# Graph layer on one core: row and node one-hots in one VectorE instruction, row one-hots widened by ScalarE

## The chip, the cores and the metric

The kernel runs on one core of a Trainium2 chip. The metric is the device time of one execution in microseconds (us). The core has TensorE (PE, with its weight loads shown apart as PEld), VectorE (DVE), ScalarE (ACT), GpSimd (POOL) and SyncE (SP), and 16 DMA engines that all of them feed.

## The reference, cut to what matters

6250 nodes with 256 features, 200000 weighted edges. A layer norm is followed by a sum over edges (the part that the change touches), an attention-like product and, after a second layer norm, a mixture of eight experts:

```
xn = layernorm(x)
msgs = edge_weight[:, None] * xn[dst]            # for each edge, a row of 256
agg = segment_sum(msgs, src, num_segments=6250)  # added up by node
x = x + agg + mix(xn)
x = x + moe(layernorm(x))
```

## The kernel before

The stages run one after another: the norm, the mix, the edge stage, the routing, the experts. The edge stage takes some 1350 us of the 1988.

The edges are cut into 7 rounds (`q`, NQ = 7), and within a round each of 49 steps (`b`, NB = 49) treats one block of 128 nodes; a step has the number `t = q * 49 + b`. For a step there are six tiles of up to 128 edges. Three (GN) have rows of `xn` fetched by GpSimd, one indirect DMA each (L1285). Three (DN) have edges whose rows lie close together, in a window of 128 rows that is already in SBUF. Every tile is turned into a matrix product: a one-hot of the edge's node times its weight says to which node the row goes.

What the engines do in step `t`:

- VectorE makes the one-hots of the step (`one_hots`). L1440 compares the numbers 0 to 127, each written twice side by side in PSUM (`slots_of`), with the node of each edge (`recb`, six numbers a step and partition): 6 x 128 bf16, `hots`. L1445 compares the same numbers, fp32 in PSUM, with the row of each edge within its window (`recd`, three a step): 3 x 128 fp32, `row_hots`. Both write one of two buffers, by `t % 2`. L1458 (`finish`) adds the finished product of an earlier step to the node's sum.
- ScalarE (`weigh`, L1388) multiplies the six node one-hots by the edge weights, one instruction each, bf16 to fp32, into `weighted`. It also moves the window products from PSUM to SBUF (`keep`, L1379).
- TensorE makes `ap`, the row one-hots times the weighted node one-hots (L1338, which needs `weighted_done`), then the products of the fetched rows (L1351, which needs the gathers and VectorE's `summed` of two steps before), then those of the windows (L1355, which needs ScalarE's `a_kept`).
- GpSimd may be up to five steps (AHEAD) in front of TensorE.

In rounds 1 to 6 the next round is also sorted beside the products (`bins`): VectorE counts and places edges (`dve_share`; among it L445, L489, L511 and L513), TensorE multiplies what it made (L392), ScalarE moves the result (L405). At the end of a round `dve_decode` writes `recb`, `recd` and `scale` for the next one (L579 to L581). In the last round the sorting is gone, and the second layer norm and the routing run beside the products.

The order on every engine is that of the code. VectorE's turn in step `b` is: one-hots of step `b + 1`, then L1458 for step `b - 2`, then its share of the sorting. ScalarE's turn is: `keep` of step `b`, then `weigh` of step `b + 1`. Before the one-hots VectorE waits for two events, so that the buffer that it overwrites has been read: `a_done` (TensorE has used `row_hots`) and `weighted_done` (ScalarE has used `hots`).

Of the kernel before, what the change touches and what calls it, by code (L numbers as in the profile page):

```python
# [12 lines left out]
ALU = mybir.AluOpType  # L13
# [3 lines left out]
P = 128  # L17
# [12 lines left out]
NB = NT  # L30
# [76 lines left out]
class Bins:  # L107
# [4 lines left out]
    FARTHEST = 254  # L112
    NE = SC
    assert NE % 2 == 0
    HALVES = 2 * CB
# [20 lines left out]
    def __init__(self, nc, st, above, iota49, iota128, part, ident, low_i):  # L136
# [43 lines left out]
        self.recb = st.sb("recb", [P, NB, NE], BF16)  # L180
        self.recd = st.sb("recd", [P, NB, DN])
        self.scale = st.sb("scale", [P, NB, SC])
# [93 lines left out]
    def dve_consts(self, dve):  # L276
        nc = self.nc
        nc.vector.memset(self.ones[:, :], 1.0)
        nc.vector.memset(self.ones_f[:, :], 1.0)
        nc.vector.memset(self.offset[:, 0, :], 0.0)  # L280
        nc.vector.memset(self.merged[:, :, GN, :], 0)
        for i in range(2):
            nc.vector.tensor_copy(self.iota128b[:, :, i], self.iota128[:, :])
            last = nc.vector.tensor_copy(self.iota49b[:, :, i], self.iota49[:, :])
        self.link(dve, last)
# [286 lines left out]
    def dve_decode(self, dve, q):  # L572
        nc = self.nc

        if q > 0:
            dve.wait_ge(self.weighted_done, q * NB)
        for a, b, node, weight in ((0, GN, self.merged[:, 1, 0:GN, :], self.merged[:, 2, 0:GN, :]),
                                   (GN, SC, self.src_of[:, KG:CB, :], self.weight_of[:, KG:CB, :])):
            nc.vector.tensor_copy(self.recb[:, :, a:b], node.rearrange("p k b -> p b k"))  # L579
            nc.vector.tensor_copy(self.scale[:, :, a:b], weight.bitcast(F32).rearrange("p k b -> p b k"))  # L580
        nc.vector.tensor_scalar_add(self.recd[:, :, :], self.dst_of[:, KG:CB, :].rearrange("p k b -> p b k"), -1.0)\  # L581
            .then_inc(self.decoded, 1)
        dve.wait_ge(self.decoded, q + 1)
        assert self.links == self.LINKS, self.links
# [582 lines left out]
def edge_stage(nc, xn_dram, sum_dram, low_i, flag, h, ident, iota128, bins, router_w, rwT, logits, hn_dram):  # L1167


    with Stage(nc, "edge") as st:  # L1170
        NE, AHEAD = bins.NE, 5
        recb, recd, scale = bins.recb, bins.recd, bins.scale
        most1 = st.sb("most1", [P, 1])
# [5 lines left out]
        hots = st.sb("hots", [P, 2, NE // 2, P, 2], BF16)  # L1179
        row_hots = st.sb("row_hots", [P, 2, DN, P])  # L1180
        weighted = st.sb("weighted", [P, 2, SC, P])
# [60 lines left out]
        with nc.Block() as block:  # L1242
# [128 lines left out]
            def _(act):  # L1371
# [9 lines left out]
                def weigh(q, b):  # L1381
# [3 lines left out]
                    if t >= 2:  # L1385
                        act.wait_ge(stepped, t - 1)
                    for i in (*range(GN, SC), *range(GN)):
                        last = nc.scalar.activation(weighted[:, t % 2, i, :], hots[:, t % 2, i // 2, :, i % 2], ACT.Copy,  # L1388
                                                    scale=scale[:, b, i:i + 1])
# [43 lines left out]
            def _(dve):  # L1433
                def one_hots(q, b):

                    t = q * NB + b
                    if t >= 2:
                        dve.wait_ge(a_done, t - 1)
                        dve.wait_ge(weighted_done, t - 1)
# [3 lines left out]
                        recb[:, b, :].rearrange("p (t a h) -> p t a h", a=1, h=2).to_broadcast([P, NE // 2, P, 2]),  # L1443
                        ALU.is_equal)
                    nc.vector.tensor_tensor(  # L1445
                        row_hots[:, t % 2, :, :],
                        rows_of_window[:, :].rearrange("p (a s) -> p a s", a=1).to_broadcast([P, DN, P]),
                        recd[:, b, :].rearrange("p (c a) -> p c a", a=1).to_broadcast([P, DN, P]),
                        ALU.is_equal).then_inc(hot_done, 1)
# [976 lines left out]
```

## Time and profile before

| what | value |
|---|---|
| median of three runs | 1996.81 us (1991.59 to 1999.81) |
| the profiled execution | 1989.69 us, its span 1988.0 us |
| busy share PE / PEld / DVE / ACT / POOL | 89% / 77% / 69% / 55% / 65% |
| GpSimd's gathers L1285 | 1029, from 271.2 us on |
| mean granted TensorE clock | 0.956 of 2.4 GHz |

A row of a timeline gives the start of an instruction or of a merged row of like ones, how long it took, engine, line, operation, what is written and read, the count, and in brackets how long the engine had been idle and what ended that. A row of a group gives the count, the busy time, the mean of one in ns, and the idle time of the engine just before them. Matmuls are pipelined, so the starts of weight loads (PEld) are used here to tell when TensorE gets to a piece of work.

### The profile page before, as it was taken

The numbers are of one execution on the slowest core, as the hardware profiler recorded it, in microseconds if no ns is written. First come the engines' busy times: TensorE is split into PE (matmuls) and PEld (weight loads), VectorE is DVE, ScalarE is ACT, GpSimd is POOL, SyncE is SP. The second block draws the span as 40 slices with busy tenths as digits, with TensorE's granted clock in tenths as the row PEclk, the third lists the DMA queues.
The fourth block names the chain that finished last, engine by engine and source line by source line (L and its number), as shares of the span: only waits on it lengthen the run. The fifth ranks groups of instructions, "written<-read, shape, count | busy, mean of one in ns | idle before, by whom it ended". The sixth has DMA issues, their size and how long they took to land. (4 is left out here: it accounts for less than half of the span.)

```text
span 1988.0 us, 33518 instructions
## 1 busy us (share of the span) xinstructions
PE 1764.5 (89%) x10522; PEld 1527.8 (77%) x10522; DVE 1380.9 (69%) x2880; ACT 1093.2 (55%) x3267; POOL 1286.6 (65%) x1283
## 2 busy tenths in 40 slices
PE   5677878999899989998999999999999983999994
PEld 3366667988798889887988898889899972787773
DVE  6988458886888798788878986988677768010113
ACT  5632025556555655565556555655576652776662
POOL 1000367777777777777777777777777740777773
PEclk9988889999999999999999999999999986999997
DMA  7522453443233323332333333333344432344557
GB/s 255 196 87 95 138 173 122 139 131 117 91 107 104 112 91 106 105 112 90 105 105 108 93 107 104 104 99 104 106 133 133 136 109 70 102 144 131 164 161 228
DMA packets 130054, 244.30 MB, mean 123 GB/s; under 512 B 26533, under 2 KB 77620, under 8 KB 129880
## 3 DMA queue, kind: packets, MB, share of 16 engines
q0 software_dynamic: 59584, 161.78, 26.9%
q1 hardware_dynamic: 63852, 73.97, 11.4%
q10 hardware_dynamic: 6444, 6.40, 0.9%
q8 instruction: 89, 1.46, 0.3%
q14 instruction: 85, 0.70, 0.1%
HBM read 197.24 MB, written 45.77 MB: 122 GB/s over the span
## 5 line engine op out<-in xcount | busy, mean ns | idle before, releaser
L1285 POOL DMA_INDIRECT edge_G<-xn_scratch,edge_row_i x1029 | 1031.7, 1003 | 313.5 <-issue 290.6
L1388 ACT ACTIVATE edge_weighted<-edge_hots,bins_scale 128x128 f32<-128x128 bf16 x2058 | 638.5, 391 | 66.6 <-DVE edge_row_hots L1445 65.3
L1351 PE MATMUL edge_op<-edge_G,edge_weighted 128*128 128x256 f32 x2058 | 523.9, 391 | 62.1 <-DVE all_xn L1458 36.7
L1379 ACT COPY edge_A<-edge_ap 128x384 f32<-128x384 f32 x343 | 164.1, 478 | 533.1 <-PE edge_ap L1338 533.1
L1351 PEld LDWEIGHTS edge_op<-edge_G,edge_weighted 128*128 128x128 f32 x2058 | 366.7, 191 | 111.2 <-DVE all_xn L1458 50.7
L1440 DVE TENSOR_TENSOR edge_hots<-edge_numbers,bins_recb 128x768 bf16<-128x768 bf16 x343 | 190.6, 556 | 194.2 <-PE edge_ap L1338 190.0
L1338 PEld LDWEIGHTS edge_ap<-edge_weighted,edge_row_hots 128*128 128x128 f32 x2058 | 278.7, 192 | 39.1 <-issue 14.2
L1338 PE MATMUL edge_ap<-edge_weighted,edge_row_hots 128*128 128x128 f32 x2058 | 287.5, 276 | 11.6 <-ACT edge_weighted L1388 8.7
L1355 PE MATMUL edge_op<-bins_win,edge_A 128*128 128x256 f32 x1176 | 289.9, 383 | 0.0
L1355 PEld LDWEIGHTS edge_op<-bins_win,edge_A 128*128 128x128 f32 x1176 | 226.8, 193 | 31.9
L1355 PE MATMUL edge_op<-edge_win,edge_A 128*128 128x256 f32 x882 | 218.4, 384 | 0.0
L2320 DVE SCALAR_TENSOR_TENSOR exp_acc<-exp_ys,ffn_share,all_xn 128x256 f32<-128x256 f32 (+1 forms) x49 | 20.6, 481 | 248.9 <-DMA exp_ys<-ys_scratch 246.8
L1355 PEld LDWEIGHTS edge_op<-edge_win,edge_A 128*128 128x128 f32 x882 | 170.6, 193 | 24.2
L1445 DVE TENSOR_TENSOR edge_row_hots<-edge_numbers,bins_recd 128x384 f32<-128x384 f32 x343 | 187.8, 548 | 0.0
L1080 POOL TENSOR_TENSOR all_xn<-mix_xg,mix_qbias 128x1024 f32<-128x1024 f32 (+1 forms) x13 | 29.0, 2228 | 188.8 <-DVE mix_xg L1158 187.7
L392 PE MATMUL bins_bp<-bins_RH,bins_SL 128*128 128x147 bf16 x1582 | 142.0, 232 | 8.5 <-DVE bins_SL L513 8.0
L2184 POOL DMA_INDIRECT exp_xt<-hn_scratch,ffn_token x105 | 103.0, 981 | 71.6 <-POOLq L2007 40.0
L1458 DVE TENSOR_TENSOR all_xn<-all_xn,edge_op 128x256 f32<-128x256 f32 (+1 forms) x343 | 140.9, 411 | 9.0 <-PE edge_op L1355 8.8
L392 PEld LDWEIGHTS bins_bp<-bins_RH,bins_SL 128*128 128x128 bf16 x1582 | 122.4, 99 | 12.8 <-DVE bins_SL L513 7.5
L2190 POOL DMA_INDIRECT ys_scratch<-exp_yt,ffn_target x105 | 108.0, 1028 | 32.3 <-issue 28.3
L2239 PE MATMUL exp_dn<-ffn_w2s,exp_gT 128*128 x420 | 120.1, 409 | 0.0
L2226 PE MATMUL exp_up<-exp_xT,exp_w1x 128*128 128x128 f32 x840 | 113.6, 279 | 0.1
(343 smaller groups left out, 2080.2 us busy)
## 6 DMA issues: line engine op xcount, KB each, us to landing
edge_G<-xn_scratch,edge_row_i POOLq DMA_INDIRECT x1029
exp_ys<-ys_scratch SPq DMA_DIRECT2D x12, 1024.0 KB, 6.4
ln_xin<-in_x SPq DMA_DIRECT2D x12, 512.0 KB, 5.3
xn_scratch<-ln_xnb ACTq DMA_DIRECT2D x12, 512.0 KB, 6.3
xnT_scratch<-ln_xT SPq DMA_DIRECT2D x12, 512.0 KB, 6.8
mix_xg<-xn_scratch SPq DMA_DIRECT2D x12, 512.0 KB, 3.8
mix_ek<-xnT_scratch SPq DMA_DIRECT2D x12, 512.0 KB, 4.7
mix_xg<-in_x SPq DMA_DIRECT2D x12, 512.0 KB, 3.9
```

The source lines that it names most:

```text
L392: last = nc.tensor.matmul(self.bp[:, 0:self.NV * NB], self.SL[:, s % 2, t - a, :, side], self.R[:, s % 2, t - a, :, :, side].rearrange("p ...
L1285: pool.indirect_dma_start(out=G[:, t % AHEAD, i, :], out_offset=None, in_=xn_dram, in_offset=bass.IndirectOffsetOnAxis(ap=row_i[:, q % 2, ...
L1338: last = nc.tensor.matmul(ap[j][:, i * P:(i + 1) * P], row_hots[:, j, i, :], weighted[:, j, GN + i, :], start=True, stop=True)
L1351: nc.tensor.matmul(op[j][:, :], weighted[:, j, i, :], G[:, rb, i, :], start=i == 0, stop=False)
L1355: last = nc.tensor.matmul(op[j][:, :], A[:, j, i, :], win[q % 2][:, i, :], start=False, stop=i == DN - 1)
L1379: nc.scalar.copy(A[:, j, :, :].rearrange("p c s -> p (c s)"), ap[j][:, :]).then_inc(a_kept, 1)
L1388: last = nc.scalar.activation(weighted[:, t % 2, i, :], hots[:, t % 2, i // 2, :, i % 2], ACT.Copy, scale=scale[:, b, i:i + 1])
L1440: nc.vector.tensor_tensor(hots[:, t % 2, :, :, :], bins.slots_of[:, :, :].rearrange("p (a s) h -> p a s h", a=1).to_broadcast([P, NE // 2, ...
L1445: nc.vector.tensor_tensor(row_hots[:, t % 2, :, :], rows_of_window[:, :].rearrange("p (a s) -> p a s", a=1).to_broadcast([P, DN, P]), recd ...
L1458: nc.vector.tensor_tensor(h[:r, b, :], h[:r, b, :], op[(q * NB + b) % 2][:r, :], ALU.add).then_inc(summed, 1)
L2226: last = nc.tensor.matmul(up[t % 2][f][:, :], w1x[:, t % WB, k, f * P:(f + 1) * P], xT[:, t % 2, k, :], start=k == 0, stop=k == KC - 1)
L2239: last = nc.tensor.matmul(dn[t % 2][:, :], gT[:, t % DOWN, f, :], w, start=False, stop=f == KC - 1)
```

## The change

The row one-hots are made together with the node one-hots. `recb` gets ten numbers a step instead of six: six nodes, three rows within the window, and a tenth that is -1 throughout and matches nothing, so that the count is even. One bf16 instruction compares all ten. `recd` is gone; L581 writes into `recb`. TensorE still takes fp32 row one-hots, so ScalarE copies the last four of the ten to `row_hots` in fp32, with one instruction of 512 elements ahead of the six multiplications. It reads the pairs side by side and writes their halves into two rows of `row_hots`, 512 bytes apart. Since ScalarE now writes `row_hots`, VectorE's wait for `a_done` is dropped.

```
-    NE = SC
+    NE = SC + DN + 1
...
-        self.recd = st.sb("recd", [P, NB, DN])
...
+        nc.vector.memset(self.recb[:, :, self.NE - 1:self.NE], -1.0)
...
-        nc.vector.tensor_scalar_add(self.recd[:, :, :], self.dst_of[:, KG:CB, :].rearrange("p k b -> p b k"), -1.0)\
+        nc.vector.tensor_scalar_add(self.recb[:, :, SC:SC + DN], self.dst_of[:, KG:CB, :].rearrange("p k b -> p b k"), -1.0)\
...
-        row_hots = st.sb("row_hots", [P, 2, DN, P])
+        row_hots = st.sb("row_hots", [P, 2, DN + 1, P])
...
                     if t >= 2:
                         act.wait_ge(stepped, t - 1)
+                    nc.scalar.copy(row_hots[:, t % 2, :, :].rearrange("p (c h) s -> p c s h", h=2),
+                                   hots[:, t % 2, SC // 2:NE // 2, :, :])
                     for i in (*range(GN, SC), *range(GN)):
...
                     if t >= 2:
-                        dve.wait_ge(a_done, t - 1)
                         dve.wait_ge(weighted_done, t - 1)
                     nc.vector.tensor_tensor(
                         hots[:, t % 2, :, :, :],
...
-                        ALU.is_equal)
-                    nc.vector.tensor_tensor(
-                        row_hots[:, t % 2, :, :],
-                        rows_of_window[:, :].rearrange("p (a s) -> p a s", a=1).to_broadcast([P, DN, P]),
-                        recd[:, b, :].rearrange("p (c a) -> p c a", a=1).to_broadcast([P, DN, P]),
                         ALU.is_equal).then_inc(hot_done, 1)
```

On VectorE, at steps 12 to 14 of a round, where the sorting adds (L489) between the steps' own instructions, there stand before:

```order
L489 TENSOR_TENSOR bins_BH<-bins_BH,bins_start 128x4802 [waits bins_chain]
L1440 TENSOR_TENSOR edge_hots<-edge_numbers,bins_recb 128x768 [waits bins_weighted_done,edge_a_done]
L1445 TENSOR_TENSOR edge_row_hots<-edge_numbers,bins_recd 128x384
L1458 TENSOR_TENSOR all_xn<-all_xn,edge_op 128x256 [waits edge_stepped]
L489 TENSOR_TENSOR bins_BH<-bins_BH,bins_start 128x5488
L489 TENSOR_TENSOR bins_BH<-bins_BH,bins_start 128x2x392
L1440 TENSOR_TENSOR edge_hots<-edge_numbers,bins_recb 128x768 [waits bins_weighted_done,edge_a_done,bins_chain]
L1445 TENSOR_TENSOR edge_row_hots<-edge_numbers,bins_recd 128x384
L1458 TENSOR_TENSOR all_xn<-all_xn,edge_op 128x256 [waits edge_stepped]
L489 TENSOR_TENSOR bins_BH<-bins_BH,bins_onehot 128x4802
```

And on VectorE at the same place now (L1440 has become L1441, L1458 has become L1454):

```order
L489 TENSOR_TENSOR bins_BH<-bins_BH,bins_start 128x4802 [waits bins_chain]
L1441 TENSOR_TENSOR edge_hots<-edge_numbers,bins_recb 128x1280 [waits bins_weighted_done]
L1454 TENSOR_TENSOR all_xn<-all_xn,edge_op 128x256 [waits edge_stepped]
L489 TENSOR_TENSOR bins_BH<-bins_BH,bins_start 128x5488
L489 TENSOR_TENSOR bins_BH<-bins_BH,bins_start 128x2x392
L1441 TENSOR_TENSOR edge_hots<-edge_numbers,bins_recb 128x1280 [waits bins_weighted_done,bins_chain]
L1454 TENSOR_TENSOR all_xn<-all_xn,edge_op 128x256 [waits edge_stepped]
L489 TENSOR_TENSOR bins_BH<-bins_BH,bins_onehot 128x4802
```

One instruction is gone between two additions, the other is longer, and the wait for `edge_a_done` is gone.

On ScalarE, from the first steps of the edge stage on, there stand before:

```order
L1379 COPY edge_A<-edge_ap 128x384 [waits edge_a_done]
L1388 ACTIVATE edge_weighted<-edge_hots,bins_scale 128x128 [waits edge_stepped,edge_hot_done]
L1388 ACTIVATE edge_weighted<-edge_hots,bins_scale 128x128 x5
L1379 COPY edge_A<-edge_ap 128x384 [waits edge_stepped,edge_a_done]
L1388 ACTIVATE edge_weighted<-edge_hots,bins_scale 128x128 [waits edge_stepped,edge_hot_done]
```

And on ScalarE at the same place now (L1388 has become L1390):

```order
L1379 COPY edge_A<-edge_ap 128x384 [waits edge_a_done]
L1387 CAST edge_row_hots<-edge_hots 128x2x128x2 [waits edge_stepped,edge_hot_done]
L1390 ACTIVATE edge_weighted<-edge_hots,bins_scale 128x128 x6
L1379 COPY edge_A<-edge_ap 128x384 [waits edge_stepped,edge_a_done]
L1387 CAST edge_row_hots<-edge_hots 128x2x128x2 [waits edge_stepped,edge_hot_done]
```

The copy (CAST) stands between the evacuation and the six multiplications, and has taken over their wait.

## Rows read from the trace of the kernel before

**Rows 1.** Groups by line, 271 to 1618 us: count, busy us, mean ns, idle before

```profile
L1285 POOL DMA_INDIRECT edge_G<-xn_scratch,edge_row_i x1029 | 1031.7, 1003 | 313.5 <-issue 290.6 <-PE edge_op L1355 20.7 <-POOL edge_row_i L1276 2.1
...
L1351 PE MATMUL edge_op<-edge_G,edge_weighted 128*128 128x256 f32 x2046 | 520.8, 391 | 62.1 <-DVE all_xn L1458 36.7 <-DMA edge_G<-xn_scratch,edge_row_i 25.2
```

**Rows 2.** Instructions of line L1285: duration in ns, minimum, median and maximum

```profile
L1285 POOL DMA_INDIRECT edge_G<-xn_scratch,edge_row_i x1029: 942/946/3162, 271.2 to 1616.8; - x172
```

**Rows 3.** Timeline of POOL, 507 to 524 us: start, us, what, idle before

```profile
510.89 2.73 POOL L1285 DMA_INDIRECT edge_G<-xn_scratch,edge_row_i  x1 [0.31 <-issue]
513.92 0.95 POOL L1285 DMA_INDIRECT edge_G<-xn_scratch,edge_row_i  x1 [0.30 <-issue]
...
518.11 0.95 POOL L1285 DMA_INDIRECT edge_G<-xn_scratch,edge_row_i  x1 [0.30 <-issue]
...
522.54 0.95 POOL L1285 DMA_INDIRECT edge_G<-xn_scratch,edge_row_i  x1 [0.31 <-issue]
```

**Rows 4.** Timeline of DVE in the same stretch (steps 12 to 14)

```profile
510.14 2.66 DVE L489 TENSOR_TENSOR bins_BH<-bins_BH,bins_start 128x4802 bf16<-128x4802 bf16 x1
512.72 0.55 DVE L1440 TENSOR_TENSOR edge_hots<-edge_numbers,bins_recb 128x768 bf16<-128x768 bf16 x1
513.19 0.55 DVE L1445 TENSOR_TENSOR edge_row_hots<-edge_numbers,bins_recd 128x384 f32<-128x384 f32 x1
513.65 0.41 DVE L1458 TENSOR_TENSOR all_xn<-all_xn,edge_op 128x256 f32<-128x256 f32 x1
513.98 3.01 DVE L489 TENSOR_TENSOR bins_BH<-bins_BH,bins_start 128x5488 bf16<-128x5488 bf16 x1
...
518.77 2.65 DVE L489 TENSOR_TENSOR bins_BH<-bins_BH,bins_onehot 128x4802 bf16<-128x4802 bf16 x1
...
522.60 3.01 DVE L489 TENSOR_TENSOR bins_BH<-bins_BH,bins_onehot 128x5488 bf16<-128x5488 bf16 x1
```

**Rows 5.** Timelines of PEld and ACT, 1404 to 1436 us, a light step

```profile
1422.97 0.74 PEld L1338 LDWEIGHTS edge_ap<-edge_weighted,edge_row_hots 128*128 128x128 f32 x6
1423.94 0.48 ACT L1379 COPY edge_A<-edge_ap 128x384 f32<-128x384 f32 x1 [1.03 <-PE edge_ap L1338]
1424.32 1.86 ACT L1388 ACTIVATE edge_weighted<-edge_hots,bins_scale 128x128 f32<-128x128 bf16 x6
1426.23 0.74 PEld L1338 LDWEIGHTS edge_ap<-edge_weighted,edge_row_hots 128*128 128x128 f32 x6
```

**Rows 6.** The same timelines, a heavy step

```profile
1408.17 0.85 PEld L1338 LDWEIGHTS edge_ap<-edge_weighted,edge_row_hots 128*128 128x128 f32 x6
1409.63 1.86 ACT L1388 ACTIVATE edge_weighted<-edge_hots,bins_scale 128x128 f32<-128x128 bf16 x6
1412.03 0.85 PEld L1338 LDWEIGHTS edge_ap<-edge_weighted,edge_row_hots 128*128 128x128 f32 x6
```

**Rows 7.** Timeline of PEld, 1494 to 1508 us, two steps of the last round

```profile
1499.94 0.85 PEld L1338 LDWEIGHTS edge_ap<-edge_weighted,edge_row_hots 128*128 128x128 f32 x6
1503.87 0.85 PEld L1338 LDWEIGHTS edge_ap<-edge_weighted,edge_row_hots 128*128 128x128 f32 x6
```

**Rows 8.** The page, costliest groups: the two one-hot instructions

```profile
L1440 DVE TENSOR_TENSOR edge_hots<-edge_numbers,bins_recb 128x768 bf16<-128x768 bf16 x343 | 190.6, 556 | 194.2 <-PE edge_ap L1338 190.0
...
L1445 DVE TENSOR_TENSOR edge_row_hots<-edge_numbers,bins_recd 128x384 f32<-128x384 f32 x343 | 187.8, 548 | 0.0
```

**Rows 9.** Timeline of DVE, 740 to 748 us: a longer comparison of the same kind

```profile
740.15 1.35 DVE L513 TENSOR_TENSOR bins_SL<-edge_numbers,bins_slot 128x2304 bf16<-128x2304 bf16 x1
```

**Rows 10.** Groups of ACT by shape: a copy of 512 elements in the last stage

```profile
L2249 ACT COPY exp_w1x<-ffn_w1s 128x512 f32 x105 | 64.9, 618 | 33.1 <-issue 25.7 <-PEq L2007 7.4
```

**Rows 11.** Instructions of line L580, which reads its input 196 bytes apart

```profile
L580 DVE COPY bins_scale<-bins_merged x7: 236/237/238, 265.9 to 1432.9; 128x147 f32<-128x147 f32 x7
```

**Rows 12.** Timeline of PEld, 1370 to 1398 us: TensorE waits for VectorE's sum

```profile
1395.90 1.16 PEld L1351 LDWEIGHTS edge_op<-edge_G,edge_weighted 128*128 128x128 f32 x6 [1.06 <-DVE all_xn L1458]
```

More of the change, by code:

```diff
@@ L112 @@
     FARTHEST = 254
-    NE = SC
-    assert NE % 2 == 0
+    NE = SC + DN + 1
+    assert SC % 2 == 0 and DN == 3
     HALVES = 2 * CB
@@ L1171, in edge_stage @@
         NE, AHEAD = bins.NE, 5
-        recb, recd, scale = bins.recb, bins.recd, bins.scale
+        recb, scale = bins.recb, bins.scale
         most1 = st.sb("most1", [P, 1])
```

## The prediction

> **What bounds the kernel now.** I read the per-line groups of the edge stage first. GpSimd issues 1029 row gathers there, 3 in each of 343 steps (7 rounds of 49). They are busy 1031.7 us with 313.5 us between them, and nearly all of those gaps are put down to plain issue [rows 1]: 1345 us from start to end, so GpSimd is never held up by the rest. A gather's median is 0.946 us [rows 2] and the next starts 0.30 us later; 1029 times 1.25 is 1287 us. The other 58 us are stalls, and the timeline shows what they are. A gather that starts while an L489 addition of VectorE is running, one with both sources in SBUF, ends 0.82 us after that addition does: the addition from 510.14 ends at 512.80, the gather from 510.89 at 513.62 [rows 3, 4]. A gather that starts just before the addition is not touched: the one at 513.92 keeps its 0.95 us though L489 begins at 513.98 and lasts to 516.99. The one-hots L1440 and L1445, with one source in PSUM, run in every step and delay nothing that the median shows.
>
> TensorE has almost the same pace, in two kinds of step. In a light step (no sorting products) the weight load of L1338 starts 0.05 us after ScalarE's six L1388 end: 1426.18 against 1426.23 [rows 5]. The step is then a ring: evacuation L1379 (0.38 us until L1388 starts), L1388 (1.86), 0.05, the products L1338, and the next evacuation 0.04 after them; 3.26 us from load to load. A heavy step takes 3.86 us and there the weights are ready 0.54 us early: L1388 from 1409.63 ends at 1411.49, the load starts at 1412.03 [rows 6]. In the last round, without sorting but with routing, steps take 3.93 us [rows 7]. Comparing the end of L1388 with the next L1338 load over all steps, 13 of 49 in rounds 2 to 6 are light, 4 in the last; nearly all others have 0.46 to 0.61 us to spare. TensorE waits for late sums of VectorE 36.7 us and for gathers only 25.2 us in all [rows 1], the latter at steps 12 to 15 of a round, right after the long gathers.
>
> **The change, part by part.** *VectorE.* L1440 rises from 768 to 1280 elements. Between 768 elements at 0.556 us [rows 8] and L513's 2304 at 1.35 us [rows 9], same types and also with a PSUM source, an element costs 0.517 ns, so 1280 take 0.82 us. L1440 and L1445 now start 0.47 us apart, and L1458 follows L1445 after 0.46 [rows 4]; together 0.93 us become 0.74: 0.2 us saved a step, 70 us over the stage, none of it on GpSimd's chain. The wait for a_done that falls away lets the one-hots start earlier, but L1458 behind them still waits for the step's sum. The memset, the assembly of recb and the dropped recd are about equal and happen once a round.
>
> *ScalarE.* One copy of 512 elements, bf16 to fp32, goes in front of L1388. Nearest row: L2249, SBUF to SBUF, 512 elements, 0.618 us [rows 10]; consecutive instructions overlap by 0.10 (L1379 lasts 0.48 and L1388 starts 0.38 after it [rows 5]). It adds 0.52 us to the ring, 178 us of busy time. Queued behind it are the six L1388, and TensorE waits for their last. Light steps go from 3.26 to 3.78; heavy ones need 0.52 + 0.05 of their 0.54, so they lose 0.03. The lower bound is the 0.38 us for which L1379 with 384 elements holds the engine. The upper one is 1.04, twice 0.52, if the writes, which alternate between two rows 512 bytes apart, ran at half rate. The nearest row with a stride, VectorE's L580 (reading 196 bytes apart), takes 237 ns for 147 elements [rows 11], no sign of half rate; I take 0.52.
>
> The Trainium skill ("SBUF — State Buffer", Door 1: The DMA port swizzle) says that SBUF has lines of 16 bytes and that each access that crosses to a new line pays a penalty. The copy's writes cross at every element, so by that rule it would lie nearer the upper bound, with the time of rival 2 instead of the sum below. No run here shows it for a write.
>
> *Where the 0.52 goes.* Per round about 7.5 us are added (13 light steps at 0.52, the rest in tenths and hundredths). In rounds 1 to 6 this is covered: the gathers set the time of steps 12 to 15, TensorE arrives there with some 3.6 us of waiting to spare (25.2 over seven rounds), and up to 5 us of waiting for VectorE (36.7 over seven) shrinks as VectorE gets quicker. Step 38 of round 6 is such a place: 1.06 us idle for L1458 [rows 12]. Gather pace, 1345/343 = 3.92 us, is above 3.78 and about equal to the heavy steps. After step 15 of round 6 nothing covers: 8 steps with 0.05 to 0.07 us of slack cost 4.2 us, the remaining ones 2. Against that, steps 36 to 40 of round 6, held by VectorE, give back between 0 and 4; I take 2.4. Tail: **+4 us** (2 to 6).
>
> *Where VectorE's 0.2 us goes.* This is the part that costs. Each round has four large L489 additions, with one pair of one-hots and L1458 between them. From the end of the first (512.80) to the start of the second (513.98) are 1.18 us [rows 4]; the stalled gather ends 0.82 after the first and the next starts 0.30 later, at 513.92, 0.06 us ahead [rows 3]. With 0.2 us less between the additions the second starts at 513.78, 0.14 us before that gather, which is then held until the addition ends. One gather slot of 1.25 us is lost. The same 0.06 us lead stands before the fourth addition (522.54 against 522.60); the third has 0.66 (518.11 against 518.77) and keeps its free gather. Two slots a round are 2.5 us. Against that the series itself is 3 times 0.2 us shorter, and the first long gather (2.73 here) can come out between 2.2 and 3.4 by where it falls. Per round I take +1.5 (1 to 2.5), over six rounds **+9 us** (6 to 15).
>
> Sum: 4 + 9 = **+13 us** on the profiled 1989.69 us (span 1988.0), 2002.7. The median of the runs shown is 7.1 us above that profile; on 1996.81 the change gives **2010 us**.
>
> **Rivals.**
> 1. *The gathers aren't held more* (not slower): the order of gather and addition does not flip, or a gather doesn't mind an addition that started so shortly before. Only the tail is left: +4 us, 2001. For it: the lead is 0.06 us, and everything else must stay in step. Against: starts 0.1 us before a gather do stall one elsewhere in this stage, and the pattern repeats in all rounds. The Trainium skill ("SBUF — State Buffer", Who interferes with whom) infers that a tensor_tensor does not stop descriptor generation. By that rule this rival would hold; the 2.73 us gather speaks against it.
> 2. *The copy costs more than the ring can hide* (slower by more). From 0.66 us (3.92 less 3.26) the ring replaces GpSimd as the bound in every step. At 0.75 it takes 4.01 us, times 343 is 1375: +30 us (2027); at 1.04, 4.30 us, +130 us (2127). For it: no ScalarE row writes with such a stride. Against: rows 11, and that L2249 with the same count fits. Its like is an L1440 that loses its two elements a cycle: 0.16 us of start-up (0.556 less 768 times 0.517 ns) and L1445's 1.01 ns an element (0.548 less 0.16, over 384) make 1.46 us, and VectorE would be late in most heavy steps, some +30 us.
> 3. *Faster*: VectorE's shorter series also falls well for the gathers, all four long ones shrink to about 2 us and the sums are never late. Up to 58 us of stall are there, but VectorE's additions remain; -12 us (1985) would need a fifth of it gone.
>
> **How the numbers follow.** The forecast (+3 to +24 us) has 0.55, rival 1 0.22, rival 2 0.15, rival 3 0.08. A measurement of this kernel tells about 0.5%, 10 us, from no change. Two thirds of the forecast's cases and all of rival 2 lie above that: 0.51 slower; rival 1 and the rest of the forecast, 0.41 the same; 0.08 faster. The range runs from -3 us (1994) to +39 us (2036): it takes in the forecast, rival 1 and a copy of up to 0.75 us, and leaves out rival 3 and the doubled copy.
>
> **What would show it.** Right: L1440 near 0.82 us; the copy near 0.62 us; light steps at 3.78; gathers of about 3.7 us under the 5488-element L489, and GpSimd's stretch 6 to 15 us longer, still without waiting for TensorE. Wrong: the copy over 0.75 us; gathers waiting for L1355 for tens of us; or a stretch of 1345 us as before.

## The result and the profile after

The changed kernel takes 2070.16 us (median of 4 runs, 2068.31 to 2071.01) against 1997.26 for the kernel before on the same chip: a ratio of 1.0368, 95% interval 1.0344 to 1.0391. Forecast were 2010 us and a range to 2036. The direction was right, the size was not: 73 us came in place of 13. The profiled execution has a span of 2066.6 us.

The groups of the edge stage (273 to 1689 us; columns as in [rows 1]), to be compared with [rows 1, 8]:

```profile
L1285 POOL DMA_INDIRECT edge_G<-xn_scratch,edge_row_i x1029 | 1036.8, 1008 | 377.1 <-issue 257.1 <-PE edge_op L1355 117.6 <-POOL edge_row_i L1276 2.5
L1387 ACT CAST edge_row_hots<-edge_hots 128x512 f32<-128x512 bf16 x340 | 376.0, 1106 | 49.6 <-DVE edge_hots L1441 49.6
L1351 PE MATMUL edge_op<-edge_G,edge_weighted 128*128 128x256 f32 x2034 | 507.1, 385 | 3.0 <-DMA edge_G<-xn_scratch,edge_row_i 3.0
L1441 DVE TENSOR_TENSOR edge_hots<-edge_numbers,bins_recb 128x1280 bf16<-128x1280 bf16 x341 | 280.3, 822 | 264.5 <-ACT edge_weighted L1390 261.6 <-DVE bins_found L529 0.4
L1338 PEld LDWEIGHTS edge_ap<-edge_weighted,edge_row_hots 128*128 128x128 f32 x2037 | 253.5, 191 | 224.7 <-ACT edge_weighted L1390 205.3 <-issue 19.2
```

Read the releasers first. GpSimd, which in [rows 1] was held almost only by its own issue, now waits 117.6 us for TensorE's L1355. TensorE no longer waits for sums or gathers in front of L1351 (3.0 us against 62.1), but 205.3 us for ScalarE's multiplications in front of L1338. VectorE waits for ScalarE too. All of them stand behind one engine, and its new instruction, L1387, has a mean of 1106 ns. The prediction took it to be as long as L2249, 618 ns.

A step can be followed in the weight loads of TensorE (timeline of PEld, 848 to 864 us):

```profile
858.01 0.74 PEld L1338 LDWEIGHTS edge_ap<-edge_weighted,edge_row_hots 128*128 128x128 f32 x6 [0.42 <-ACT edge_weighted L1390]
...
862.15 0.74 PEld L1338 LDWEIGHTS edge_ap<-edge_weighted,edge_row_hots 128*128 128x128 f32 x6 [0.42 <-ACT edge_weighted L1390]
```

and on ScalarE (timeline of ACT, the same stretch):

```profile
858.99 0.48 ACT L1379 COPY edge_A<-edge_ap 128x384 f32<-128x384 f32 x1 [1.02 <-PE edge_ap L1338]
859.36 1.09 ACT L1387 CAST edge_row_hots<-edge_hots 128x512 f32<-128x512 bf16 x1
860.25 1.84 ACT L1390 ACTIVATE edge_weighted<-edge_hots,bins_scale 128x128 f32<-128x128 bf16 x6
...
863.12 0.48 ACT L1379 COPY edge_A<-edge_ap 128x384 f32<-128x384 f32 x1 [1.02 <-PE edge_ap L1338]
```

This is the ring of [rows 5] with one link more: evacuation 0.37 us until the copy starts, copy 0.89 until L1390 starts, L1390 1.84, then 0.06 to the weight load and 0.97 to the next evacuation; 4.14 us from load to load, in steps with and without sorting alike. 343 steps of 4.14 us are 1420 us; at GpSimd's pace they took 1345 [rows 1]. The difference of 75 us is the loss. What the change saves on VectorE is worth nothing here, since VectorE itself waits 261.6 us for ScalarE's multiplications.

### The profile page after: what moved, and what is told of

Same layout as the page of the kernel before. It is cut to its first block and busy times, and to the rows that moved or that the text cites. A ratio compares the mean times of both kernels' runs of the same rounds, so it can differ in the third digit from the quotient of the medians.

```text
span 2066.6 us, 33262 instructions
## 1 busy us (share of the span) xinstructions
PE 1819.4 (88%) x10522; PEld 1493.5 (72%) x10522; DVE 1313.2 (64%) x2538; ACT 1392.3 (67%) x3610; POOL 1291.2 (62%) x1283
## 5 line engine op out<-in xcount | busy, mean ns | idle before, releaser
L1285 POOL DMA_INDIRECT edge_G<-xn_scratch,edge_row_i x1029 | 1036.8, 1008 | 377.1 <-issue 257.1
L1390 ACT ACTIVATE edge_weighted<-edge_hots,bins_scale 128x128 f32<-128x128 bf16 x2058 | 632.3, 389 | 0.0
L1351 PE MATMUL edge_op<-edge_G,edge_weighted 128*128 128x256 f32 x2058 | 513.2, 386 | 3.0 <-DMA edge_G<-xn_scratch,edge_row_i 3.0
L1441 DVE TENSOR_TENSOR edge_hots<-edge_numbers,bins_recb 128x1280 bf16<-128x1280 bf16 x343 | 282.0, 822 | 264.5 <-ACT edge_weighted L1390 261.6
L1338 PEld LDWEIGHTS edge_ap<-edge_weighted,edge_row_hots 128*128 128x128 f32 x2058 | 256.1, 191 | 225.8 <-ACT edge_weighted L1390 206.3
L1387 ACT CAST edge_row_hots<-edge_hots 128x512 f32<-128x512 bf16 x343 | 379.3, 1106 | 49.6 <-DVE edge_hots L1441 49.6
L1338 PE MATMUL edge_ap<-edge_weighted,edge_row_hots 128*128 128x128 f32 x2058 | 321.0, 292 | 93.5 <-ACT edge_weighted L1390 81.5
L1351 PEld LDWEIGHTS edge_op<-edge_G,edge_weighted 128*128 128x128 f32 x2058 | 365.0, 191 | 39.2 <-DMA edge_G<-xn_scratch,edge_row_i 2.3
L1355 PE MATMUL edge_op<-bins_win,edge_A 128*128 128x256 f32 x1176 | 286.8, 380 | 0.0
L1355 PEld LDWEIGHTS edge_op<-bins_win,edge_A 128*128 128x128 f32 x1176 | 224.3, 191 | 30.8
L1355 PE MATMUL edge_op<-edge_win,edge_A 128*128 128x256 f32 x882 | 214.3, 379 | 0.0
L1355 PEld LDWEIGHTS edge_op<-edge_win,edge_A 128*128 128x128 f32 x882 | 167.6, 190 | 22.8
L1454 DVE TENSOR_TENSOR all_xn<-all_xn,edge_op 128x256 f32<-128x256 f32 (+1 forms) x343 | 140.9, 411 | 16.7 <-PE edge_op L1355 16.7
```

Source lines behind the costliest of these rows:

```text
L1285: pool.indirect_dma_start(out=G[:, t % AHEAD, i, :], out_offset=None, in_=xn_dram, in_offset=bass.IndirectOffsetOnAxis(ap=row_i[:, q % 2, ...
L1338: last = nc.tensor.matmul(ap[j][:, i * P:(i + 1) * P], row_hots[:, j, i, :], weighted[:, j, GN + i, :], start=True, stop=True)
L1351: nc.tensor.matmul(op[j][:, :], weighted[:, j, i, :], G[:, rb, i, :], start=i == 0, stop=False)
L1355: last = nc.tensor.matmul(op[j][:, :], A[:, j, i, :], win[q % 2][:, i, :], start=False, stop=i == DN - 1)
L1387: nc.scalar.copy(row_hots[:, t % 2, :, :].rearrange("p (c h) s -> p c s h", h=2), hots[:, t % 2, SC // 2:NE // 2, :, :])
L1441: nc.vector.tensor_tensor(hots[:, t % 2, :, :, :], bins.slots_of[:, :, :].rearrange("p (a s) h -> p a s h", a=1).to_broadcast([P, NE // 2, ...
```

## The experiments

Theory W: ScalarE's write pattern makes the copy slow, and the copy's place on the ring (the loop of evacuation, multiplications and products that each step goes through) carries that into every step. Rivals: the type conversion (T), other engines' company in SBUF (C), or VectorE's shorter series and its effect on the gathers. The kernel before was run anew beside each of three groups of runs, and its median was 1993.7, 1993.0 and 1999.4 us; a ratio is always to the kernel before of the same group. Where runs of two groups are set side by side, differences of some 0.3% say nothing by themselves, and the stage in the traces is used too. The first group has the copy by itself, the copy row by row, the pairs and the added copy; the second the slow and the quick copy in another place, the filler in every step and the first cut; the third the rest.

### The copy by itself, in many forms

Behind the edge stage of the kernel before, once its products were done, four copies of each form:

```
+ last = nc.scalar.copy(part[n], b512)                                                        # L1441
+ last = nc.scalar.copy(part[n].rearrange("p (c h s) -> p c s h", c=2, h=2), bpairs)          # L1445
+ last = nc.scalar.copy(part[n], f512)                                                        # L1449
...
```

> The kernel before, and behind its edge stage, when the other engines are done, copies of 512 elements a partition in thirteen forms on ScalarE, four of each in a row, then three of the forms on VectorE. Theory W (the writes): an element whose place is not next to the one before costs about twice as much. Then bf16 to fp32 in sequence takes 0.62 us, the change's form (halves of pairs into two rows 512 bytes apart) 1.1 us, the same from fp32 1.1, rows written one after another with the reads 4 bytes apart 0.62, reads 256 bytes apart 0.62; runs of four elements in a row before the jump about 0.62 to 0.75. If the 16-byte line is what counts, strides of 16 and 28 bytes take 1.1 too, and 8 bytes 0.62 to 0.8; if only the going back and forth counts, all strides take 0.62. Theory T (the type): bf16 to fp32 takes 1.1 in every order, fp32 to fp32 0.62 in every order. Theory C (company): alone, with the other engines idle, the change's form takes 0.62 us like the rest, and it is slow only beside other work. The time of the whole kernel says nothing here; about 35 to 60 us are added.

Instructions by line: duration of one in ns (minimum, median, maximum), first and last start. In this order: bf16 to fp32 in sequence; the change's form; fp32 to fp32 in sequence; the change's form from fp32; bf16 to bf16 in the change's form; row by row (reads 4 bytes apart); reads back and forth between places 256 bytes apart; fp32 writes 16, 8 and 28 bytes apart; then VectorE in sequence and in the change's form.

```profile
L1441 ACT CAST edge_G<-edge_hots x4: 614/618/621, 1636.5 to 1638.1; 128x512 f32<-128x512 bf16 x4
L1445 ACT CAST edge_G<-edge_hots x4: 1073/1075/1076, 1638.7 to 1641.3; 128x512 f32<-128x512 bf16 x4
L1449 ACT COPY edge_G<-edge_row_hots x4: 612/612/617, 1642.5 to 1644.0; 128x512 f32<-128x512 f32 x4
L1453 ACT COPY edge_G<-edge_row_hots x4: 1075/1080/1082, 1644.7 to 1647.3; 128x512 f32<-128x512 f32 x4
L1457 ACT COPY edge_G<-edge_hots x4: 2445/2741/2741, 1648.4 to 1654.9; 128x512 bf16<-128x512 bf16 x4
L1461 ACT CAST edge_G<-edge_hots x4: 612/612/617, 1657.7 to 1659.2; 128x512 f32<-128x512 bf16 x4
L1465 ACT CAST edge_G<-edge_hots x4: 668/671/674, 1659.9 to 1661.6; 128x512 f32<-128x512 bf16 x4
L1469 ACT COPY edge_G<-edge_row_hots x4: 1093/1103/1105, 1662.3 to 1665.0; 128x512 f32<-128x512 f32 x4
L1473 ACT COPY edge_G<-edge_row_hots x4: 635/636/646, 1666.1 to 1667.7; 128x512 f32<-128x512 f32 x4
L1477 ACT COPY edge_G<-edge_row_hots x4: 1106/1110/1117, 1668.4 to 1671.2; 128x512 f32<-128x512 f32 x4
...
L1611 DVE CAST edge_G<-edge_hots x4: 420/421/428, 1678.8 to 1679.8; 128x512 f32<-128x512 bf16 x4
L1615 DVE CAST edge_G<-edge_hots x4: 620/621/643, 1680.2 to 1681.7; 128x512 f32<-128x512 bf16 x4
```

T falls: the conversion costs nothing (618 against 612 ns), and from fp32 the same writes cost 1080. C falls as the main cause: alone the copy takes 1075 ns, in the stage 1106. W holds: a write that does not stay near the one before costs 1075 in place of 618 ns. Going back and forth is not needed for it. Writes 16 and 28 bytes apart cost the same, writes 8 bytes apart almost nothing (636). The Trainium skill ("SBUF — State Buffer", Door 1: The DMA port swizzle) says that SBUF's lines have 16 bytes and that at least two accesses must hit a line for the full rate. For fp32 writes the rows agree with that: two a line 636 ns, one a line 1075 to 1110.

### The copy row by row

```
- nc.scalar.copy(row_hots[:, t % 2, :, :].rearrange("p (c h) s -> p c s h", h=2),
-                hots[:, t % 2, SC // 2:NE // 2, :, :])
+ nc.scalar.copy(row_hots[:, t % 2, :, :].rearrange("p (c h) s -> p c h s", h=2),
+                hots[:, t % 2, SC // 2:NE // 2, :, :].rearrange("p c s h -> p c h s"))
```

> The changed kernel with one thing else: ScalarE's copy goes through the same 512 elements row by row, so that it writes each row in sequence and reads the bf16 halves 4 bytes apart. Theory W: the copy takes 0.62 us, steps take 3.78 us in place of 4.14, TensorE again waits for GpSimd's pace, and the kernel comes to 2003 to 2012 us, which is what the prediction said of the change. Theory T: the copy stays at 1.1 us and the kernel at 2065 to 2075. If the copy is short and the kernel still stands over 2025 us, the other steps of the prediction fail too (VectorE's shorter series would cost more than 9 us).

2006.85 us against 1993.72: ratio 1.0072 (1.0055 to 1.0089). Groups of the stage (265 to 1640 us):

```profile
L1285 POOL DMA_INDIRECT edge_G<-xn_scratch,edge_row_i x1029 | 1042.3, 1013 | 313.5 <-issue 302.5 <-PE edge_op L1355 8.8 <-POOL edge_row_i L1276 2.1
L1351 PE MATMUL edge_op<-edge_G,edge_weighted 128*128 128x256 f32 x2052 | 518.7, 389 | 35.3 <-DMA edge_G<-xn_scratch,edge_row_i 27.8 <-DVE all_xn L1454 7.5
...
L1387 ACT CAST edge_row_hots<-edge_hots 128x512 f32<-128x512 bf16 x343 | 213.3, 622 | 55.2 <-DVE edge_hots L1441 55.2
```

The same elements in another order take 622 ns, a light step takes 3.79 us (loads of L1338 at 1432.42 and 1436.21), and GpSimd is the bound again (8.8 us of waiting for TensorE in place of 117.6). Of the 73 us some 60 hang on the order of two loops. What is left is +13 us, the sum of the prediction with the copy that it had assumed.

### Pairs kept together

```
- row_hots = st.sb("row_hots", [P, 2, DN + 1, P])
+ row_hots = st.sb("row_hots", [P, 2, (DN + 1) // 2, P, 2])
...
- last = nc.tensor.matmul(ap[j][:, i * P:(i + 1) * P], row_hots[:, j, i, :],
+ last = nc.tensor.matmul(ap[j][:, i * P:(i + 1) * P], row_hots[:, j, i // 2, :, i % 2],
```

> The changed kernel with row_hots kept in pairs, as hots has them: the copy reads and writes in sequence, and TensorE reads its weights 8 bytes apart. Theory W: the copy takes 0.62 us. If TensorE reads at a stride of 8 bytes as fast as in sequence, the kernel comes to the time of the row by row copy, 2003 to 2012 us. If it pays a like price for the stride, the L1338 products take up to twice as long (0.98 to about 1.9 us from first load to the end), the ring gains 0.4 to 0.9 us and the kernel stands at 2060 to 2250 us. Theory T: the copy takes 1.1 us, 2065 us and more.

2009.11 us, ratio 1.0075 (1.0059 to 1.0092), not to be told from the copy row by row. The copy takes 622 ns here too. TensorE's six weight loads of L1338 take 0.78 us in place of 0.74 with the reads 8 bytes apart. So here, where the reads are 4 bytes apart (ScalarE) or 8 (TensorE), the jumps can be put on the reading side at almost no cost.

### The copy alone added to the kernel before

```
+ extra = st.sb("extra", [P, 2, 4, P])
...
+ nc.scalar.copy(extra[:, t % 2, :, :].rearrange("p (c h) s -> p c s h", h=2),
+                hots[:, t % 2, 0:2, :, :])
  for i in (*range(GN, SC), *range(GN)):
```

> The kernel before, VectorE and all, with one more ScalarE copy a step ahead of the six multiplications, in the change's form (512 elements, bf16 to fp32, halves of pairs into two rows 512 bytes apart), into a tile that nobody reads. The ring theory (only ScalarE's copy counts: keep 0.38, copy 0.89, six products 1.84, products and the way there 1.03, 4.14 us a step times 343 is 1420 against 1345): 2065 to 2075 us, like the changed kernel, with steps of 4.14 us. If VectorE's new one-hots and the gathers take a share of the 73 us: 2045 to 2060. If the copy is hidden here: under 2010, and the loss is VectorE's.

2079.15 us, ratio 1.0425 (1.0407 to 1.0442). VectorE's and GpSimd's code is that of the kernel before, and the loss is there in full, and a little more than expected. Two groups of this kernel (265 to 1700 us; its lines are shifted by a few):

```profile
L1388 ACT CAST edge_extra<-edge_hots 128x512 f32<-128x512 bf16 x340 | 376.5, 1107 | 58.3 <-DVE edge_row_hots L1448 58.3
...
L1443 DVE TENSOR_TENSOR edge_hots<-edge_numbers,bins_recb 128x768 bf16<-128x768 bf16 x341 | 189.3, 555 | 243.9 <-PE edge_ap L1339 239.8 <-DVE bins_BH L439 0.9
```

Its steps without a stop also take 4.14 us. Some are longer, since the one-hots are late for the copy (58.3 us in all, 49.6 in the changed kernel). VectorE waits for TensorE's use of `row_hots` (L1339) before them, the wait that the change drops, and its own series is longer; which of the two makes them late was not separated. The 9 us over the changed kernel are what the rest of the change gives back where the ring is the bound.

### The slow copy in another place

The copy as the change has it, for step b + 1, issued ahead of the evacuation of step b, where ScalarE stood idle for 1.02 us:

```
- nc.scalar.copy(row_hots[...], hots[...])        # in weigh, ahead of the six multiplications
...
  for b in range(NB):
+     widen(q * NB + b + 1)                       # the same copy, behind its wait for hot_done
      keep(q, b)
      weigh(q, b + 1)
```

> The changed kernel, copy and all (1.1 us, halves into two rows), with one thing else: ScalarE issues the copy of step b+1 ahead of its keep of step b, where it has waited about 1.0 us for TensorE's products (329.9 us in all before L1379 in the changed kernel). The ring theory says that what costs is the copy's place on the ring, not ScalarE's busy time or the copy's traffic in SBUF: 0.89 us fit into the 1.03 us from the end of the six products to keep, light steps come back to about 3.3 us, GpSimd's pace sets the time again and the kernel comes to 2000 to 2015 us. If the one-hots are often late, keep behind the copy is late with them, 2015 to 2045. If the writes disturb other engines wherever the copy stands, 2060 to 2070 as before.

2000.82 us, ratio 1.0033 (1.0019 to 1.0047). Timeline of ACT, 850 to 866 us:

```profile
853.10 1.86 ACT L1391 ACTIVATE edge_weighted<-edge_hots,bins_scale 128x128 f32<-128x128 bf16 x6
854.86 1.09 ACT L1383 CAST edge_row_hots<-edge_hots 128x512 f32<-128x512 bf16 x1
855.98 0.48 ACT L1379 COPY edge_A<-edge_ap 128x384 f32<-128x384 f32 x1
856.36 1.86 ACT L1391 ACTIVATE edge_weighted<-edge_hots,bins_scale 128x128 f32<-128x128 bf16 x6
```

The slow copy is all there, but it lies under TensorE's products, and the step takes 3.26 us, as in [rows 5]. The same instruction costs some 67 us more in the change's place than here (1.0368 less 1.0033; the medians differ by 69).

### The quick copy in that place

The same move with the copy row by row.

> The same place for the copy, and the copy row by row (0.62 us). If the prediction's two terms hold (tail +4 for ScalarE's copy on the ring, +9 for the gathers under L489), the first goes and the second stays: 3 to 6 us under the row by row copy in its old place (2006.85), 2000 to 2004 us. If it comes down to the kernel before (1994 or less), the gathers' term wasn't real.

2000.33 us, ratio 1.0036 (1.0022 to 1.0050): no different from the slow copy there, as it must be if the idle time covers both. Against the copy row by row on the ring (1.0072) the move gives back 0.36%, some 7 us. L1285 takes 1042.5 us, as on the ring (1042.3).

### The gap between the additions made long again

```
+ nc.vector.tensor_tensor(filler[:, t % 2, :], rows_of_window[:, 0:112],
+                         scale[:, b, 0:1].to_broadcast([P, 112]), ALU.is_equal)
  nc.vector.tensor_tensor(hots[...], ...)
```

> The row by row copy in the change's place, and on VectorE a comparison of 112 numbers ahead of the one-hots, into a tile that nobody reads, so that the one-hots again take about 0.93 us between two L489 additions instead of 0.74. If the gathers' term is what the prediction said (with 0.2 us less between the additions, the second of each pair starts before a gather, and holds it 2.7 us longer), the 3.69 us gathers disappear, the L1285 sum falls from 1042 to about 1031, and the kernel from 2006.85 to 1996 to 2000 us, though VectorE does more. If the term isn't real, it stays at 2005 to 2010.

2007.15 us, ratio 1.0076 (1.0059 to 1.0093): no gain, although the 3.7 us gathers are gone. Groups of this kernel:

```profile
L1286 POOL DMA_INDIRECT edge_G<-xn_scratch,edge_row_i x1029 | 1028.0, 999 | 323.1 <-issue 285.8 <-PE edge_op L1356 35.3 <-POOL edge_row_i L1277 2.1
L1352 PE MATMUL edge_op<-edge_G,edge_weighted 128*128 128x256 f32 x2052 | 519.2, 389 | 34.5 <-DVE all_xn L1457 28.6 <-DMA edge_G<-xn_scratch,edge_row_i 6.0
```

The expectation (1996 to 2000) was missed. Most of GpSimd's gain of 14 us returned as waiting: TensorE waits for VectorE's sums (28.6 us against 7.5), and GpSimd for TensorE (35.3 against 8.8). The filler was in all 343 steps, the additions need it in three a round. So the trial was repeated with it there alone:

```
+ if q + 1 < NQ and bins.SLOT_AT + 1 < b <= bins.SLOT_AT + 4:
      nc.vector.tensor_tensor(filler[...], ...)
```

> The row by row copy in the change's place, with the filler comparison of 112 numbers only ahead of the three one-hots a round that stand between the L489 additions, not in every step. In every step it undid the flip (gathers 1042.3 to 1028.0 us, none of 3.7) but made VectorE's sums late for TensorE (waits for L1457 63.5 us against 16.2 for L1454), and the time stayed at 2007. If the gathers' term is real and only that second wait hid it: L1285 near 1030 us, and the kernel at 1995 to 2000. If the gathers' term is worth nothing in time: 2005 to 2010 again, with the shorter gathers.

1999.76 us against 1999.38, ratio 1.0006 (0.9997 to 1.0016). Groups of this kernel:

```profile
L1286 POOL DMA_INDIRECT edge_G<-xn_scratch,edge_row_i x1029 | 1032.7, 1004 | 313.5 <-issue 302.2 <-PE edge_op L1356 9.1 <-POOL edge_row_i L1277 2.1
```

VectorE does 18 comparisons more, and the gathers take 9.6 us less than without them (1032.7 against 1042.3) with the same time between them. The kernel is 7 us quicker by its median and 13 by the ratios (1.0006 against 1.0072); the two runs stand in different groups. The starts of the gathers (first and last) and of VectorE's sums tell it apart, one profiled execution each: the kernel before (its gathers are in [rows 2]), the copy row by row on the ring, the same early, and the three fillers a round.

```profile
L1458 DVE TENSOR_TENSOR all_xn<-all_xn,edge_op x343: 404/410/422, 285.9 to 1626.0; 128x256 f32<-128x256 f32 x168, 106x256 f32<-106x256 f32 x4
...
L1285 POOL DMA_INDIRECT edge_G<-xn_scratch,edge_row_i x1029: 942/946/3688, 273.3 to 1629.6; - x172
L1454 DVE TENSOR_TENSOR all_xn<-all_xn,edge_op x343: 407/410/423, 286.2 to 1643.4; 128x256 f32<-128x256 f32 x168, 106x256 f32<-106x256 f32 x4
...
L1285 POOL DMA_INDIRECT edge_G<-xn_scratch,edge_row_i x1029: 942/946/3688, 274.3 to 1630.5; - x172
L1458 DVE TENSOR_TENSOR all_xn<-all_xn,edge_op x343: 403/410/424, 287.4 to 1638.4; 128x256 f32<-128x256 f32 x168, 106x256 f32<-106x256 f32 x4
...
L1286 POOL DMA_INDIRECT edge_G<-xn_scratch,edge_row_i x1029: 942/946/3237, 275.2 to 1621.9; - x172
L1458 DVE TENSOR_TENSOR all_xn<-all_xn,edge_op x343: 407/410/423, 287.8 to 1635.7; 128x256 f32<-128x256 f32 x168, 106x256 f32<-106x256 f32 x4
```

| kernel | first to last gather, us | last gather to last sum, us |
|---|---|---|
| before | 1345.6 | 9.2 |
| row by row, on the ring | 1356.3 | 13.8 |
| row by row, early | 1356.2 | 7.9 |
| on the ring, three fillers a round | 1346.7 | 13.8 |

The gathers' term of the prediction is real in time: it is the first column, and the fillers take it away. The second column is the tail, and the early copy takes that away.

### The additions cut into pieces

L489, the source of the long gathers, in pieces of two rows, on top of the quick copy in the early place:

```
- for a, b, w in ((0, cut, CB),) if part_ == 0 else ((cut, SP2, CB), (SP2, LP, KG)):
+ whole = ((0, cut, CB),) if part_ == 0 else ((cut, SP2, CB), (SP2, LP, KG))
+ for a, b, w in [(i, min(i + 2, b), w) for a, b, w in whole for i in range(a, b, 2)]:
```

> early_rowwise, with each L489 addition cut into pieces of two rows (1372 elements, some 0.8 us), the same sums. A gather that starts under an addition has ended 0.82 us after the end of that one instruction, also where the next followed at once (before: gather 515.17 to 517.81, addition to 516.99, the next from 516.91). If so, gathers under L489 take 0.9 to 1.7 us in place of 2.6 to 3.7, some 30 us of stall are gone from GpSimd's 1345, and as TensorE's steps of 3.3 and 3.85 us let it follow, the kernel comes to 1970 to 1990 us, faster than both. If a gather needs a gap between instructions, not the end of one, it stays at early_rowwise's time; if VectorE, with more instructions, is late for TensorE, 2005 to 2020.

1964.59 us, ratio 0.9861 (0.9844 to 0.9877), faster than both kernels and below the expected range. The kernel before with the cut alone:

> The kernel before, with the L489 additions cut into pieces of two rows, and nothing of the change. It tells how much of the 28 us that the split version with the early copy gained comes from the cut alone. If GpSimd's stalls are the bound of the kernel before, as the prediction read it, the stalls under L489 fall here too (gathers 1031.7 to about 1005 us) and the kernel comes to 1965 to 1975. If the dropped a_done wait and the cheaper one-hots have a share of the gain, 1975 to 1990.

1981.05 us, ratio 0.9914 (0.9897 to 0.9931). It lies in the second range of its expectation, for the case that the rest of the change has a share in the gain; as the kernel before took 1999.4 us in this group, the range alone does not show that. And the first of them with single rows:

> The early row by row copy with L489 cut into single rows (686 elements, about 0.5 us) in place of two. A gather under a piece then ends at most 0.5 + 0.82 us after the piece began: 1.3 in place of up to 1.7, some 5 us less stall. If VectorE has the time, 1957 to 1963 us; if its longer series (some 0.05 us for each of 13 more pieces in a round and addition pair) is late for TensorE, 1965 to 1972.

1960.79 us, ratio 0.9808 (0.9792 to 0.9825), the best of this study. Groups of the kernel before with the cut into two rows:

```profile
L1286 POOL DMA_INDIRECT edge_G<-xn_scratch,edge_row_i x1029 | 998.2, 970 | 332.5 <-issue 284.6 <-PE edge_op L1356 45.9 <-POOL edge_row_i L1277 2.1
L1352 PE MATMUL edge_op<-edge_G,edge_weighted 128*128 128x256 f32 x2058 | 520.4, 389 | 61.1 <-DVE all_xn L1459 58.2 <-DMA edge_G<-xn_scratch,edge_row_i 2.9
```

of the changed kernel with the same cut and the quick copy early:

```profile
L1286 POOL DMA_INDIRECT edge_G<-xn_scratch,edge_row_i x1029 | 1003.1, 975 | 313.5 <-issue 298.0 <-PE edge_op L1356 13.4 <-POOL edge_row_i L1277 2.1
L1352 PE MATMUL edge_op<-edge_G,edge_weighted 128*128 128x256 f32 x2058 | 517.4, 388 | 40.3 <-DMA edge_G<-xn_scratch,edge_row_i 33.2 <-DVE all_xn L1459 6.8
```

and of the last one:

```profile
L1286 POOL DMA_INDIRECT edge_G<-xn_scratch,edge_row_i x1029 | 996.0, 968 | 313.7 <-issue 301.2 <-PE edge_op L1356 10.4 <-POOL edge_row_i L1277 2.1
L1352 PE MATMUL edge_op<-edge_G,edge_weighted 128*128 128x256 f32 x2058 | 516.7, 387 | 39.1 <-DVE all_xn L1459 32.2 <-DMA edge_G<-xn_scratch,edge_row_i 6.6
```

The gathers are nearly equally short, but with the old one-hots TensorE waits 58.2 us for VectorE's sums and GpSimd 45.9 for TensorE; with the new ones and the same cut 6.8 and 13.4, with single rows 32.2 and 10.4. Here, once GpSimd's stalls are gone, the change's side on VectorE is worth something at last: with the same cut into two rows, 0.9861 against 0.9914. The two stand in different groups, but the waits agree with it. Whether the shorter one-hots or the dropped wait for `a_done` does it was not separated. Where a gather falls under a piece (timelines of POOL and DVE of the last kernel; the second row merges seven pieces):

```profile
506.34 1.29 POOL L1286 DMA_INDIRECT edge_G<-xn_scratch,edge_row_i  x1 [0.30 <-issue]
```

```profile
506.29 3.07 DVE L490 TENSOR_TENSOR bins_BH<-bins_BH,bins_start 128x686 bf16<-128x686 bf16 x7
```

it takes 1.29 us, though six more pieces follow at once; under the whole addition it took 2.3 to 3.7.

### A second set of copies

Eleven more forms behind the edge stage of the kernel before, built like the first set.

> The kernel before with a second set of ScalarE copies behind its edge stage, four of each, the other engines done: bf16 to bf16 in sequence; with the reads 4 bytes apart; with the writes going back and forth between two places after 2, 4 and 8 elements; with writes 8, 16 and 28 bytes apart; then 192 elements of fp32 read 16 bytes apart, in sequence, and written 28 bytes apart. In the first set the going back and forth after each element cost fp32 1.08 us and bf16 2.74. If what costs is leaving a 16-byte line, two bf16 elements a line cost about half of that, four (8 bytes) a quarter, eight nothing; writes 16 and 28 bytes apart cost the full 2.5 to 2.7, 8 bytes apart half. If bf16 pays for every write of less than 4 bytes, pairs in a row (4 bytes) are as cheap as the sequence (0.62). Reads 16 bytes apart cost less than writes: 0.35 to 0.4 us for 192 elements, as in sequence; the write 28 bytes apart 0.53.

Instructions by line: bf16 to bf16, back and forth after every two elements; bf16 writes 8 bytes apart, and 16; 192 elements of fp32 read 16 bytes apart, in sequence, written 28 bytes apart.

```profile
L1449 ACT COPY edge_G<-edge_hots x4: 623/624/633, 1643.3 to 1644.9; 128x512 bf16<-128x512 bf16 x4
...
L1461 ACT COPY edge_G<-edge_hots x4: 1322/1382/1383, 1650.0 to 1653.3; 128x512 bf16<-128x512 bf16 x4
L1465 ACT COPY edge_G<-edge_hots x4: 2452/2750/2751, 1654.7 to 1661.2; 128x512 bf16<-128x512 bf16 x4
...
L1473 ACT COPY edge_G<-edge_win x4: 521/521/527, 1673.0 to 1674.3; 128x192 f32<-128x192 f32 x4
L1477 ACT COPY edge_G<-edge_win x4: 346/346/351, 1674.8 to 1675.6; 128x192 f32<-128x192 f32 x4
L1481 ACT COPY edge_G<-edge_win x4: 534/540/541, 1676.0 to 1677.0; 128x192 f32<-128x192 f32 x4
```

Two misses. By the line of 16 bytes, pairs of bf16 side by side were to cost half of 2.74 us; they cost nothing (624 ns), as in the other case that the expectation named, a price on every write of less than 4 bytes. Neither case covers both this and the writes 8 bytes apart, which cost half (1382 ns). Reads 16 bytes apart were to be free and cost nearly as much as the writes (521 against 346 ns), though the reads back and forth between two places were cheap (671 against 618). The rest came as expected.

## Why the prediction failed, point by point

- *What bounds the kernel before*: right. Shorter gathers alone make it faster (0.9914). What stood close behind it, VectorE's sums, was seen, but not that they would take back half or more of such a gain (gathers 33.5 us shorter, the kernel some 18 quicker). One reading was too narrow: of the heavy steps in rounds 2 to 6 about two thirds have 0.46 to 0.61 us to spare, the rest mostly more; nothing hangs on it.
- *VectorE*: right. L1441 takes 822 ns, forecast 0.82. The additions follow each other more closely, and the order flipped as forecast: in the changed kernel a gather from 529.07 takes 3.69 us under the addition from 528.92 (timelines of POOL and DVE, after; the second row merges the long addition and the short one behind it):

```profile
529.07 3.69 POOL L1285 DMA_INDIRECT edge_G<-xn_scratch,edge_row_i  x1 [0.30 <-issue]
```

```profile
528.92 3.48 DVE L489 TENSOR_TENSOR bins_BH<-bins_BH,bins_start 128x5488 bf16<-128x5488 bf16 x2
```

- *The gathers' term*, +9 us (6 to 15): right in size, 10.7 us from first to last gather without the slow copy (1356.3 less 1345.6), of which the three fillers a round take away 9.6. It costs the changed kernel nothing that can be seen, since GpSimd waits there anyway: the added copy alone, without the flip, lost as much. The inference quoted from the Trainium skill ("SBUF — State Buffer", Who interferes with whom), that a tensor_tensor leaves descriptor generation alone, cannot be carried over to these gathers: under L489 they take 2.3 to 3.7 us in place of 0.95. A gather also reads its row numbers from `row_i` in SBUF; which part of it is held was not separated.
- **The copy, 0.52 us: this is the step that failed.** It holds the ring for 0.89 us. The count was right (in sequence, 512 elements take 618 ns, as L2249 in [rows 10]), the pattern was what mattered, and for the pattern there was no ScalarE row. The prediction drew on [rows 11], a VectorE copy that reads with a stride, for a ScalarE copy that writes with one. The upper bound, 1.04, was built on the right mechanism and was the nearer end.
- *Rival 2* is what happened, with its mechanism, place and arithmetic: above 0.66 us the ring replaces GpSimd. (3.26 + 0.89) times 343 less 1345 is 78 us; the profiled executions differ by 78.6 (2066.6 and 1988.0), the medians by 73. It had 0.15, and the range ended at a copy of 0.75 us, for which no row spoke. With the value taken (0.52) and the upper bound (1.04) on either side of the threshold of 0.66, and no row to choose between them, the range should have gone to the upper one.
- *The tail*, +4 us (2 to 6): in the row by row kernel light steps take 3.79 us (3.78 forecast), and moving that copy off the ring gives 7 us. The sum, +13, is what the kernel with a 0.62 us copy measures. In the stage the two parts add: 10.7 us between the gathers and 4.6 in the tail (13.8 less 9.2), and each goes away by itself, the first with the fillers, the second with the early copy. The ratios (+0.72%, +0.06% without the gathers' term, +0.36% without the tail) don't add up like that; they come from three groups, between which the kernel before itself moved by 6 us.

## What to carry to other kernels

Before an instruction is priced by its element count, look at the last axis of what it writes and reads: where each element was written 16 bytes or more from the one before, a ScalarE copy of 512 fp32 cost 1.08 to 1.11 us in place of 0.62, and here turning two loops was all that it took to avoid it. On a ring of engines ask where an instruction stands, not how long it takes: the same slow copy cost no more than a quick one ahead of ScalarE's wait for TensorE, and 67 us more behind it. Where GpSimd gathers, cut long VectorE additions with both sources in SBUF into pieces.

## What was not expected of the hardware

- ScalarE's bf16 writes suffer far more than fp32 ones: 512 of them back and forth, or 16 bytes apart, take 2.74 us, and 8 bytes apart 1.38, though that is two a line; fp32 with two a line takes 0.64. Two bf16 side by side before each jump cost nothing (0.62). So the rule of two accesses a line, quoted above from the Trainium skill, tells fp32's price here, not that of bf16.
- VectorE pays less for the change's form: 621 against 421 ns for 512 elements, 0.2 us in place of ScalarE's 0.46.
- A gather held by an addition ends 0.82 us or so after the one instruction under which it started, also when like ones follow without a gap (1.29 us under the first of seven pieces); this is why cutting helps.
